# Counting the edges of a graph layer in strips of 12 rows by 125 source columns in place of 25 by 250, two strips to a step

## The reference

```python
x = x + gnn(layernorm(x), edges)      # h = relu(x@W1+b1)@W2+b2;  h + segment_sum(h[dst], src)
x = x + ffn(layernorm(x))             # softmax gate, threshold, 8 experts of 512x512, weighted sum
```

## Time and profile before

| | us |
|---|---|
| median of 3 runs | 371.01 (370.05 to 372.71) |
| the profiled execution | 369.96 |
| its span, first to last instruction | 368.2 |
| PE busy, share of the span | 351.1, 95% |
| DVE busy | 314.0, 85% |
| ACT busy | 127.9, 35% |
| granted TensorE clock | 1.00 throughout |

### The profile page before, as it was taken

How to read it: one execution, slowest core, us unless ns; L and a number is a source line. 1 busy time by engine, 2 the same in 40 slices (tenths; PEclk the granted TensorE clock), 3 DMA queues, 4 the chain that set the end, 5 groups by cost and what they waited for, 6 DMA issues and landing times.

```text
span 368.2 us, 7339 instructions
## 1 busy us (share of the span) xinstructions
PE 351.1 (95%) x2542; PEld 269.7 (73%) x2542; DVE 314.0 (85%) x565; ACT 127.9 (35%) x224; POOL 56.2 (15%) x83
## 2 busy tenths in 40 slices
PE   2999999999999989999999999999999999999995
PEld 1777787656656645457767888888888888888884
DVE  6799997999999878898686888889888888888764
ACT  5844354655679502377731313003030030210000
POOL 7000000000000000063632313050140500500000
PEclk9999999999999999999999999999999999999999
DMA  8971010222222250003000003030030300000133
GB/s 223 214 239 39 16 42 29 74 68 76 79 74 78 84 170 6 0 2 121 3 0 2 0 6 112 0 116 2 1 116 2 114 2 1 2 2 0 44 119 121
DMA packets 16273, 22.06 MB, mean 60 GB/s; under 512 B 2188, under 2 KB 9235, under 8 KB 16236
## 3 DMA queue, kind: packets, MB, share of 16 engines
q1 hardware_dynamic: 15820, 21.05, 19.4%
q10 hardware_dynamic: 416, 0.53, 0.6%
HBM read 12.77 MB, written 2.56 MB: 42 GB/s over the span
## 4 chain that ended last, share of the span: by engine, by line
PE 81%; DVE 10%; issue 3%; DMA 2%; DVEq 2%; ACT 1%; ACTq 0%
PE ps_g L1220 10%; PE ps_g L1221 10%; PE ps_g L1222 10%; PE ps_w L1108 9%; PE ps_g L1070 9%; DVE split L771 3%; PE ps_g L1056 3%; PE ps_a L1220 2%; PE ps_a L1222 2%; PE ps_a L1221 2%; PE ps_w L1221 2%; PE ps_w L1222 2%; PE ps_w L1220 2%; PE ps_g L1146 2%; DVE x_sb L854 2%
## 5 line engine op out<-in xcount | busy, mean ns | idle before, releaser
L771 DVE TENSOR_TENSOR split<-places,keys 125x1536 f16<-125x1536 int16 (+2 forms) x125 | 91.0, 794 | 4.3 <-PE ps_w L1108 1.9
L944 DVE SCALAR_TENSOR_TENSOR x_sb<-ps_g,weight_s,x_sb 125x256 f32<-125x256 f32 (+1 forms) x142 | 75.1, 546 | 19.6 <-PE ps_g L1222 18.4
L1220 PE MATMUL ps_g<-wb_hi,places 128*128 128x256 f16 x212 | 57.8, 273 | 0.1
L1221 PE MATMUL ps_g<-wb_lo,places 128*128 128x256 f16 x212 | 57.8, 273 | 0.0
L1222 PE MATMUL ps_g<-wb_hi,r_sb 128*128 128x256 f16 x212 | 57.8, 273 | 0.0
L1108 PE MATMUL ps_w<-split 125*128 125x250 f16 x402 | 53.7, 270 | 2.4 <-DVE split L771 1.8
L1108 PEld LDWEIGHTS ps_w<-split 125*128 125x128 f16 x402 | 36.7, 97 | 21.0 <-DVE split L771 8.4
L1070 PE MATMUL ps_g<-late,r_sb 125*128 125x512 f32 (+3 forms) x120 | 49.3, 516 | 1.7 <-DMA late<-counts 1.7
L574 ACT ACTIVATE wb_hi<-stage 128x512 f16<-128x512 f32 x7 | 4.4, 628 | 99.1 <-PE ps_g L1222 48.8
L1220 PE MATMUL ps_g<-wb_hi,split 128*128 128x256 f16 x142 | 38.7, 273 | 0.0
L1222 PE MATMUL ps_g<-wb_hi,split 128*128 128x256 f16 x142 | 38.7, 273 | 0.0
(11 more groups left out here) (223 smaller groups left out, 665.5 us busy)
## 6 DMA issues: line engine op xcount, KB each, us to landing
stage<-in_L_ffn_W_exp_dram SPq DMA_DIRECT2D x8, 1024.0 KB, 6.0
late<-counts SPq DMA_DIRECT2D x50, 122.1 KB
x_sb<-in_x_dram SPq DMA_DIRECT2D x5, 448.0 KB, 10.3
out_dram<-x_sb SPq DMA_DIRECT2D x10, 224.0 KB
w_sb<-in_L_gnn_W_dram SPq DMA_DIRECT2D x2, 512.0 KB, 10.0
out_dram<-x_sb ACTq DMA_DIRECT2D x10, 26.0 KB
b_sb<-in_L_gnn_b_dram SPq DMA_DIRECT2D x1, 250.0 KB
x_sb<-in_x_dram ACTq DMA_DIRECT2D x1, 208.0 KB
```

Of the source, the lines that this page charges most:

```text
L771: nc.vector.tensor_tensor(hot[hot_at(w, p)][:, 0:n, :].rearrange("p c (k x j) -> p (c k) x j", k=SEGS, j=2), places[w % WPT][:, 0:n, :].re ...
L944: nc.vector.scalar_tensor_tensor(out=x_sb[:, i, a:z], in0=bank[0:R, at:at + z - a], scalar=weight_s[:, expert_of(u), i:i + 1], in1=x_sb[:, ...
L1220: nc.tensor.matmul(out_cols, hi_x, wb_hi[par][:, q, k, :], start=(opens and k == 0), stop=False, skip_group_check=True)
L1221: nc.tensor.matmul(out_cols, hi_x, wb_lo[par][:, q, k, :], start=False, stop=False, skip_group_check=True)
```

## The change

- The windows become strips of 12 rows, and the source is cut in ten parts of 125 (position 10·dst + src//125, low part src mod 125). A chunk's one-hot row has 2 x 126 = 252 numbers in place of 384, and its matmul 125 columns in place of 250. PE's weights are the last 128 of the 252 columns.
- Two neighbouring strips are handled in one step: one comparison each, one bank (125 columns each), one copy by ACT. There are 54 groups (`NG`), three of them with one strip.
- The tables that ACT wrote are replaced by one table of running numbers, made by GpSimd (POOL) before and during the first groups and read in slices with an access pattern of five levels; lines 488 and 493 go.
- A step holds up to 6 chunks per comparison (`CAP`). Group 0 has two fixed steps of (6, 6), group 1 one of (4, 4); the loops take (5, 5), (4, 4), then per strip 6, 5, 4, 6, 5, 4, 3, 2 chunks. Every fixed step has a ring place of its own.
- DVE loads two words per group (the second strip begins at another chunk) and carries a second register through the loop.
- Each strip has its own copy SBUF to SBUF, cut in two where it crosses a tile of 125 rows: 120 pieces of 500 bytes for a whole strip.
- The preparation works on 108 columns in place of 50. Pieces of `aggregate` follow the last group of a tile by 4 to 8 groups, column sums by 7.

```diff
-    WIN = 25
-    HI = 5
-    LO = 250
-    PART = 4
-    STEPS = ((1, (4, 4, 4, 4)), (2, (3, 3, 3, 3)), (4, (4, 4, 4, 4)), (6, (4, 4, 4)), (9, (4, 3, 3)), (18, (4, 4)),
-             (30, (3, 3)), (NW, (3, 2)))
+    WIN = 12
+    HI = 10
+    LO = 125
+    SEG = 126
+    SEGS = 2
+    NG = 54
+    CAP = 6
+    RINGS = 5
+    FIXED = ((1, 2, (6, 6)), (2, 1, (4, 4)))
+    LOOP = ((1, (5, 5)), (2, (4, 4)), (3, (6,)), (4, (5,)), (5, (4,)), (10, (6,)), (13, (5,)), (30, (4,)), (NG - 1, (3,)),
+            (NG, (2,)))
...
+        def windows_of(g):
+            return (2 * g,) if g in (0, 1, NG - 1) else (2 * g, 2 * g + 1)
+        def row_of(v):
+            return WIN * (v // 2) if v < 4 else WIN * (v - 2)
+        def hot_at(stage, p):
+            return 2 * (stage % 4) + p
...
-            for w in range(NW):
-                sp.wait_ge(win_out, w + 1)
-                sp.dma_start(a_t[i % 3][q * WIN:(q + 1) * WIN, :].rearrange("p (h l) -> p h l", h=HI),
-                             counts[q][0:WIN * HI, :]).then_inc(win_moved[q], 16)
+            for g in range(NG):
+                sp.wait_ge(win_out, g + 1)
+                for s, a, z, tile, at in MOVES[g]:
+                    sp.dma_start(a_t[tile % 3][at:at + z - a, :].rearrange("p (h l) -> p h l", h=HI),
+                                 counts[q][SHIFT + a * HI:SHIFT + z * HI, s * LO:(s + 1) * LO]).then_inc(win_moved[q], 16)
...
+            def table(a, z):
+                nc.gpsimd.iota(places_all[:, a:z], pattern=[[1, z - a]], base=a, channel_multiplier=0,
+                               allow_small_or_imprecise_dtypes=True).then_inc(places_ready, 1)
...
             def block_out(g):
-                act.wait_ge(win_moved[q], 16 * (w // WPT))
+                act.wait_ge(win_moved[q], MOVED[g - RINGS])
                 act.wait_ge(win_done, g + 1)
-                nc.scalar.activation(counts[q][:, :], ps_w[w % 2][:, 0:LO], ACT.Copy).then_inc(win_out, 1)
-                if w + WPT < NW:
-                    positions(w + WPT)
+                cols = LO * len(windows_of(g))
+                nc.scalar.activation(counts[q][:, 0:cols], ps_w[g % 2][:, 0:cols], ACT.Copy).then_inc(win_out, 1)
...
+            def places_of(v, n):
+                base = places_all[0:EP, 0:SEG]
+                return bass.AP(base.tensor, base.offset, [list(base.ap[0]), [0, n], [row_of(v) * HI, SEGS], [2, SEG // 2], [1, 2]])
...
-                dve.wait_ge(pos_ready, w + 1)
+                dve.wait_ge(places_ready, table_part(g))
+                if len(windows) == 2:
+                    dve.reg_mov(at_reg, dve.snap(other_reg))
...
-                with dve.Fori(word % WORD, word // WORD, sum(parts) * REC) as k:
-                    one_step(k, 0)
-                    dve.reg_load(word_reg, wtab[0:1, w + 1:w + 2])
-                    step_done()
+                with dve.Fori(word % WORD, word // WORD, step) as k:
+                    one_step(stage, parts, (k, dve.snap(at_reg)) if len(windows) == 2 else (k,))
+                    if g + 1 < NG:
+                        dve.reg_load(word_reg, wtab[0:1, g + 1:g + 2])
+                        dve.reg_load(other_reg, wtab[0:1, 2 * NG + g + 1:2 * NG + g + 2])
+                    if len(windows) == 2:
+                        dve.reg_add(at_reg, at_reg, step)
+                    step_done()
...
                     for p, (s, n) in enumerate(parts):
                         for c in range(n):
-                            mm = nc.tensor.matmul(bank[:, 0:LO], hot[hot_at(w, p)][:, c, 0:SEG], hot[hot_at(w, p)][:, c, SEG:SEG + LO],
+                            mm = nc.tensor.matmul(bank[:, s * LO:(s + 1) * LO], one_hots[:, c, HOT - 128:HOT], one_hots[:, c, 0:LO],
                                                   start=False, stop=False, skip_group_check=True)
```

More of the change, by code:

```diff
@@ L175, in gnn_moe @@
         rstd1 = sb("rstd1", [R, TILES])
-        xn = [sb(f"xn{i}", [R, D]) for i in range(2)]
         XTS = 4
@@ L185, in gnn_moe @@
         a_sum = late[0:R, 3 * SW:4 * SW]
+        below, above, hit = (late[0:ROWS, k * GJ * NV:(k + 1) * GJ * NV].rearrange("p (j v) -> p j v", j=GJ) for k in range(3))
+        hit_idx = late[0:ROWS, 3 * GJ * NV:5 * GJ * NV].rearrange("p (a j v) -> p a j v", a=2, j=GJ)
         assert KD * N <= 4 * SW
@@ L767, in one_step @@
                         key_at = nc.s_assert_within(
-                            k + (sum(parts[:p]) - ahead) * REC, 0, (CH + PADS - n) * REC,
-                            skip_runtime_bounds_check_because="the table gives a block only steps that begin below CH")
+                            at[s] + sum(m for r, m in parts[:p] if r == s) * REC, 0, (CH + PADS - n) * REC,
+                            skip_runtime_bounds_check_because="a window's steps begin at or behind its first chunk and the pads hold all others")
@@ L1034, in _ @@
             for a in range(3):
-                row = nc.tensor.matmul(ps_a[0:1, a * NW:(a + 1) * NW], wcols[:, a:a + 1], ident[0:NW, 0:NW], start=True, stop=True)
+                row = nc.tensor.matmul(ps_a[0:1, a * NV:(a + 1) * NV], wcols[:, a:a + 1], ident[0:NV, 0:NV], start=True, stop=True)
             row.then_inc(wrows_ready, 1)
-            for p in range(4):
+            for p in range(2):
                 pe.sem_inc(hot_used[p], 1)
@@ L1111, in one_step @@
                     pe.reg_add(turn_reg, turn_reg, 1)
-                for f in range(fixed_of(w)):
-                    one_step()
+                stage = stage_of(g)
+                steps, parts = fixed_of(g)
+                for f in range(steps):
+                    one_step(stage, parts)
+                    stage = stage + 1
                     next_slot()
-                with pe.Fori(0, pe.value_load(wtab[0:1, NW + w:NW + w + 1])):
-                    one_step()
+                with pe.Fori(0, pe.value_load(wtab[0:1, NG + g:NG + g + 1])):
+                    one_step(stage, loop_of(g))
             pe.wait_ge(self_ready, 3)
-            for w in range(NW):
-                count(w)
-                if w < WPT + LAG:
-                    nc.tensor.matmul(ps_w[w % 2][:, 0:2], zeros[0:1, 0:128], zeros[0:1, 0:2], start=False, stop=True,
+            begins = [LAST[i] + LAG for i in range(TILES)]
+            pieces = {}
+            for i in range(TILES - 1):
+                for n in range(len(cuts)):
+                    pieces.setdefault(begins[i] + min(n, 4), []).append((i, n))
+            for g in range(NG):
+                count(g)
+                if g not in pieces:
+                    nc.tensor.matmul(ps_w[g % 2][:, 0:2], zeros[0:1, 0:128], zeros[0:1, 0:2], start=False, stop=True,
                                      skip_group_check=True).then_inc(win_done, 1)
@@ L1126, in _ @@
                 else:
-                    piece = (w - WPT - LAG) % WPT
-                    aggregate((w - WPT - LAG) // WPT, piece, piece + 1 if piece < WPT - 1 else len(cuts), closes=w)
-            aggregate(TILES - 2, WPT - LAG, len(cuts))
+                    i, n = pieces[g][0]
+                    aggregate(i, n, n + len(pieces[g]), closes=g)
+            for g in sorted(pieces):
+                if g >= NG:
+                    aggregate(TILES - 2, pieces[g][0][1], pieces[g][-1][1] + 1)
             aggregate(TILES - 1, 0, 2)
```

379 lines of the change are left out of this document (203 added, 176 removed).

## The result

The changed kernel takes 388.27 us in the median of four runs (386.26 to 392.2), the kernel before 370.86 us beside it: a ratio of 1.048, with a 95% interval of 1.043 to 1.053 (the ratio leaves out the run of 392.2 us, which lies over 1.5% above the fastest of the four). Forecast were 381 us, slower with a chance of 0.63, and a range of 364 to 396. Direction and range held; the median lies 7 us above the forecast.

What follows compares the result with a forecast made beforehand. PE, DVE and DVE's queue were taken as near one another, the queue binding after the change: +12.4 us to the last comparison and -2.1 in the tail on 369.96 gave 380.3, median 381, range 364 to 396.

Steps and rivals of the forecast that it cites:

- The step that decides: DVE's queue over the other 49 groups: a second load makes 1.92 us a group, last comparison at 141 us, +12.4 us.
- The load's price: Register loads in DVE's queue: 0.40 us each plus 0.03 gap, two a group, between 0.31 calm and 0.50 beside copies.
- the rival of calm loads: DVE's loads stay undisturbed: 1.72 us a group, last comparison at 131, total +0.6, 372 us; chance 0.17.
- SP: Issuing strip copies from group 5 on: 0.74 us an issue, 82 us in all, 1.68 a group, hidden under 1.92.
- the preparation: Before the first comparison: larger operations, table and second first load, +1.7 us; POOL's remaining running numbers at nothing, range 0 to 2.
- The first groups: Groups 0 to 4: DVE's work -9.2 us, preparation +1.7, second turns +2.4; DVE's queue through with group 4 at 47 us.
- The engines' terms: Comparisons on DVE fall from 89.2 to 70.6 us; counts on PE from 43.0 to 26.2, at 0.055 us each.
- the half-pace rival: The table's five-level pattern slows DVE's comparisons to 1.04 ns a number: 410 us; chance 0.05.
- The tail: After the last comparison: the last column sum's 2.13 us wait for the last copy goes, -2.1 us.

Runs made afterwards that it cites:

- two issuers: The changed kernel with the copies of each second strip issued from ScalarE's queue, those of first strips by SyncE as before: 387.03 us, ratio 1.048.
- The late table: The changed kernel with GpSimd writing the two later parts of the running numbers only once the word table is ready: 381.32 us, ratio 1.035.
- the early marks: Changed kernel, later table parts delayed, one load a group, second strips copied from ScalarE, end marks and first table part written at 2 us: 372.64 us, 1.008; first comparison 15.36.
- the kernel with both edits: The changed kernel with one register load a group (second strips compare wrong chunks) and second strips' copies issued from ScalarE's queue: 380.49 us, ratio 1.032.
- the best is at 1.016: Changed kernel computing everything with one packed word a group, later table parts delayed, marks written early, second strips copied from ScalarE's queue: 375.35 us, ratio 1.016.
- the kernel with one load: The changed kernel without VectorE's second register load in each group, so second strips compare the wrong chunks: 390.06 us, ratio 1.057.

## Why the prediction was right, and where its sum was off

- **The step that decides was right.** "Both relieved engines wait for the queue": DVE's queue with two loads one behind the other sets the group, at 1.84 us from group 5 to the last comparison ((148.0 - 57.6) / 49), for 1.92 forecast. The kernel with a load added to the kernel before shows the mechanism by itself: 11.5 us slower.
- **The load's price was too high.** A load was put at 0.40 us as disturbed by the copies. It takes 0.31, with twice as many copies as before; the queue's floor is 1.75 us, near the 1.72 of the rival of calm loads. The longer periods, most of them with a column sum, bring the mean to 1.84, so this step was nearly 4 us too dear. The sum had no term for them, and without them it would have been 8 us too dear. The rival had the load right; its 372 us failed by 10.6 us at the start and by 6 us in these periods.
- **SP was sized too low.** 0.74 us an issue, 1.68 a group, "hides under 1.92". It is 0.815 from issue to issue and, with the 106 copies of that sum, 1.76 a group, beside a queue with a floor of 1.75 and a mean of 1.84: level, not hidden. It costs the changed kernel little by itself (two issuers: nothing), but it takes away the whole gain of every repair of the queue.
- **The failed term is the preparation.** "The rest runs beside the comparisons of groups 0 and 1; I price that at nothing, with 0 to 2 us for the range." The first comparison is 10.2 us late, not 1.7. The late table shows 6.1 us of it, the early marks 2.2 (both measured by moving one thing), and what is left, 15.36 against 13.68, is 1.7, the price forecast for larger tiles and table (the kernel of 15.36 lacks the second first load, 0.2 us by 17.75 against 17.56). The prediction priced POOL's iotas on POOL only, and did not ask which of DVE's instructions run beside them.
- **The first groups.** Through group 4 the queue needed until 57.6 us, forecast 47: 8.5 us of this is the late start against 15.4. The other 2 go with the clock: the kernel with the late table, where the clock stays at 1.00, gains 6.1 us at the start and 8.2 by group 5. PE had nothing to do from 18.8 to 22.8 us while DVE was held, and then the granted clock fell:
```profile
18.80:22.80 4.00, 0.00 (x0) 0.00 (x0) 3.90 (x2) 0.00 (x0) 3.85 (x1) 1.00 0.33 88
22.80:28.00 5.20, 3.32 (x22) 2.94 (x23) 4.15 (x6) 0.59 (x1) 0.00 (x0) 0.63 0.85 259
28.00:31.40 3.40, 3.40 (x10) 2.71 (x10) 3.32 (x8) 1.17 (x3) 0.00 (x0) 0.57 0.59 225
```
  Eight matmuls of the first layer took 3.36 us at 27.99 us, and 1.95 at 32.70 when the clock was back.
- **The engines' terms held.** Comparisons at full pace (75.2 us busy, 70.6 forecast; the relief is 15.8 us and not 18.6), so the half-pace rival falls. Twelve counts of 125 columns take 0.82 us, less a tail of 0.22 and over 11 these are 0.055 us each, as forecast. By the Trainium skill (TensorE: Matmul & The Clock Gate, Back-to-back issue gap) it would be some 81 ns: this trace differs. For the load of a register, where the Trainium skill (DMA: Bandwidth & Descriptors, Latency and other measured facts) gives about 600 ns as a floor, the changed kernel's trace has medians of 310 and 308.
- **The tail** got 2.8 us shorter, 2.1 forecast, though by another way: SyncE's last copy is later than ever, but DVE has more left to do beside it.
- The sum: +10.6 by group 4, -3.7 over 49 groups and -0.7 in the tail make the +6.2 us between 380.3 forecast for the profiled execution and 386.5. That the miss is no larger is partly luck: loads priced too dear took back a third of what the start had missed.

## What to carry to other kernels

Before an engine's work is made smaller, add up what its queue does per step (loads of registers, register arithmetic, waits, branch): once the instructions are shorter than that sum, every operand that must be looked up costs its full 0.3 us, and a trace with both engines "full" can hide a queue that is nearly level with them, as here. Count the issues of copies in the same way; with two limits of one height, a repair of either alone showed no gain here, so test the pair. And a long write of GpSimd is not free because GpSimd is idle: look at which VectorE instructions run beside it, and put it beside ones that aren't held, as here by a single wait for 6 us.

In the kernel with both edits the chain runs over PE and its evictions, with DVE full in half of the stretch; none of those tried is faster than the kernel before. The best one, at 1.008, leaves out the second strips' own places; of those that compute everything the best is at 1.016. Whether a leaner queue with two loads, or a third issuer beside a short queue, would get below 1 was not tried.

## Not expected of the hardware

- Two iotas of GpSimd, 11040 numbers together, held a cast of 54 numbers for 6.5 us, over the border between them. A scaling of 80x500 took 2.47 us beside a memset and an iota, and 0.41 without them.
- A register load takes 0.31 us beside a VectorE that is busy for all of 30 us, and beside a copy every 0.815 us. In the kernels with 25-row windows it took 0.49 us in the median and up to 1.2; the cause is open.
- 4 us without work for TensorE were followed by 8.6 us at a mean granted clock of 0.57 to 0.63, and in the kernel with one load a wait of 3 us lies in 20 us granted at 0.86 and 0.80: such a hole in PE's work was paid a second time. In the changed kernel PE was idle for 11.5 of the 86 us from 62 to 148 in short pieces, and the clock stayed at 1.00.
- A copy of 12 rows issued from SyncE takes 772 ns, from ScalarE 782, from GpSimd 570.
